# Making the source masks of an edge-count stage on GpSimd instead of VectorE

## The reference

```python
edge_index = jnp.stack([src, dst])
x = layernorm(x + L0(x, edge_index))   # encoder 1024->512->256, 3 layers with
                                       #   agg = segment_sum(h[src], dst); z = h + agg, decoder
x = layernorm(x + L1(x, src, dst))     # 2 layers: h @ W_self + (agg * deg_inv) @ W_neigh + b
```

## Time and profile before

| | |
|---|---|
| median of 3 runs | 1109.51 us (1109.46 to 1112.61) |
| the profiled execution | 1108.93 us, span 1107.1 us |
| mean granted TensorE clock | 0.959 |
| PE busy | 1019.6 us, 92% of the span |
| DVE busy | 532.7 us, 48% |
| ACT busy | 351.0 us, 32% |
| POOL busy | 260.8 us, 24% |

### The profile page before, as it was taken

One profiled execution on the slowest core, in us unless ns is written; L12 is line 12 of the kernel. 1 busy time (PEld: TensorE's weight loads), 2 busy tenths in 40 slices (PEclk: granted clock), 3 DMA queues, 4 the chain that ended last, 5 costly groups with the idle time before them and its releaser, 6 DMA issues.

```text
span 1107.1 us, 14813 instructions
## 1 busy us (share of the span) xinstructions
PE 1019.6 (92%) x4862; PEld 822.2 (74%) x4862; DVE 532.7 (48%) x1314; ACT 351.0 (32%) x632; POOL 260.8 (24%) x314
## 2 busy tenths in 40 slices
PE   4787899798988599899999999999999999999996
PEld 2455668787887478777777777778887777877775
DVE  7968674455747678633222333221334234234545
ACT  5435542233424457622111222111431101222222
POOL 3000000473222533174200706001506102400000
PEclk9688898899998799999999999999999999999998
DMA  5197754299000358431322303332533433202534
GB/s 196 39 208 155 129 142 76 93 206 194 0 21 1 134 199 276 138 118 53 122 98 98 109 0 92 115 136 72 166 108 100 145 117 117 95 1 88 178 122 135
DMA packets 48263, 127.13 MB, mean 115 GB/s; under 512 B 17775, under 2 KB 18784, under 8 KB 48016
## 3 DMA queue, kind: packets, MB, share of 16 engines
q1 hardware_dynamic: 33910, 85.18, 26.3%
q0 software_dynamic: 8000, 27.02, 9.9%
q10 hardware_dynamic: 6298, 14.21, 3.8%
HBM read 101.76 MB, written 45.13 MB: 133 GB/s over the span
## 4 chain that ended last, share of the span: by engine, by line
PE 77%; DVE 8%; ACT 5%; DMA 4%; issue 3%; SPq 1%; POOL 1%; ACTq 0%; DVEq 0%; POOLq 0%
PE bank L1693 40%; PE bank L1714 17%; PE bank L1043 5%; PE bank L1075 4%; PE bank L1400 4%; DMA x_rows<-x 4%; PE bank L613 3%; ACT xt_f L260 1%; DVE stats L380 1%; PE bank L1381 1%; PE bank L1414 1%; DMA w_f<-W_pairs 1%; DVE wide L933 1%; ACT z_new L854 1%; POOL h_f L792 1%
## 5 line engine op out<-in xcount | busy, mean ns | idle before, releaser
L1634 DVE TENSOR_TENSOR h_stage<-h_turned,h_stage 128x1000 fp32r<-128x1000 f32 x80 | 104.0, 1301 | 371.9 <-ACT h_stage L1566 371.9
L1693 PE MATMUL bank<-w_self,h_stage 128*125 128x512 f32 x960 | 230.3, 395 | 0.0
L1693 PE MATMUL bank<-w_neigh,h_stage 128*125 128x512 f32 x960 | 227.0, 396 | 3.4 <-issue 3.4
L1693 PEld LDWEIGHTS bank<-w_neigh,h_stage 128*125 128x125 f32 x960 | 177.9, 186 | 47.4 <-issue 3.6
L1693 PEld LDWEIGHTS bank<-w_self,h_stage 128*125 128x125 f32 x960 | 177.9, 185 | 45.7
L1714 PE MATMUL bank<-g_rows,a_stage 125*125 125x512 f32 x800 | 192.4, 394 | 0.0
L1566 ACT ACTIVATE h_stage<-h_turned 128x1000 fp32r (+1 forms) x80 | 83.8, 1049 | 305.9 <-PE bank L1693 293.4
L1714 PEld LDWEIGHTS bank<-g_rows,a_stage 125*125 125x125 f32 x800 | 148.3, 185 | 37.6
L1531 POOL CAST w_self<-w_stage 128x512 fp32r<-128x512 f32 x32 | 22.7, 709 | 229.3 <-PE bank L1693 221.6
L1075 PE MATMUL bank<-a_turned,gn 125*128 125x418 f32 x360 | 70.5, 354 | 2.9 <-DVE gn L937 2.4
L613 PE MATMUL bank<-xt,w 128*128 128x252 f32 x480 | 63.4, 296 | 8.2 <-ACT xt_f L260 8.2
(11 more groups left out here) (204 smaller groups left out, 1162.8 us busy)
## 6 DMA issues: line engine op xcount, KB each, us to landing
a_stage<-at_dram SPq DMA_DIRECT2D x40, 625.0 KB, 4.0
w_stage<-w_self POOLq DMA_DIRECT2D x32, 256.0 KB, 3.1
at_dram<-a_turned SPq DMA_DIRECT2D x10, 625.0 KB, 9.9
w_stage<-w_neigh POOLq DMA_DIRECT2D x24, 256.0 KB, 2.9
dec_y<-x_bd SPq DMA_DIRECT2D x10, 512.0 KB, 4.2
dec_x<-x_ob SPq DMA_DIRECT2D x10, 512.0 KB, 5.3
x_dram<-h_rows SPq DMA_DIRECT2D x10, 512.0 KB, 3.8
h_dram<-o ACTq DMA_DIRECT2D x20, 256.0 KB
```

Of the source, the lines that this page charges most:

```text
L1634: dve.tensor_tensor(st[u][:, 1, :, :], ht[:, :, bass.ds(t * NT, NT)], raw(st[u][:, 0, :, :]), ALU.subtract).then_inc(st_ready, 1)
L1693: mm = pe.matmul(out, st[u][:, a, k, :], w[:, b, k * 512:(k + 1) * 512], start=(k == 0 and p == 0), stop=(k == KD - 1 and p == 2))
```

## The change

GpSimd makes the source masks of all 175 fixed visits, with the same `tensor_scalar`, and signals each on a new semaphore `sources_ready`. VectorE makes only their destination masks. TensorE waits for both before each fixed visit. The masks of the loop `more` stay on VectorE, both kinds. The slots and the rule when one is free are as before, and GpSimd now keeps to that rule too. The identity of pair p-1 is added after the source masks of pair p (the last two pairs' one after the other at the end).

```diff
+        def visit_sources(n, g, v):
+            place_src, _, slot, freed = visit_place(n // (GROUP * STATIC), n % (GROUP * STATIC))
+            if freed:
+                pool.wait_ge(hot_free, freed)
+            pool.tensor_scalar(place_src[0:EC, slot, 0:NT], iota[0:EC, 0:NT], tab[0:EC, 1, g, v:v + 1], None, ALU.is_equal)\
+                .then_inc(sources_ready, 1)
+
+        pool.wait_ge(tab_ready, 1)
+        pool.wait_ge(visit_in, 48)
+        pool.wait_ge(places_set, 3)
+        n = 0
         for p in range(PAIRS):
-            add_eye(p)
+            for j in range(GROUP):
+                for v in range(STATIC - 1):
+                    visit_sources(n, GROUP * p + j, v)
+                    n += 1
+            for j in range(GROUP):
+                visit_sources(n, GROUP * p + j, STATIC - 1)
+                n += 1
+            if p > 0:
+                add_eye(p - 1)
+        add_eye(PAIRS - 1)
...
             if freed:
                 dve.wait_ge(hot_free, freed)
-            dve.tensor_scalar(place_src[0:EC, slot, 0:NT], iota[0:EC, 0:NT], tab[0:EC, 1, g, v:v + 1], None, ALU.is_equal)
             dve.tensor_scalar(place_keys[0:EC, slot, :], iota[0:EC, :], tab[0:EC, 0, g, v:v + 1], None, ALU.is_equal)\
                .then_inc(hot_ready, 1)
...
         def count(n, j, start, stop):
+            pe.wait_ge(sources_ready, n + 1)
             pe.wait_ge(hot_ready, n + 1)
```

More of the change, by code:

```diff
@@ L120, in graph_block @@
         sem("picks"), sem("tab_ready"))
-    hot_ready, hot_free = sem("hot_ready"), sem("hot_free")
+    hot_ready, hot_free, sources_ready = sem("hot_ready"), sem("hot_free"), sem("sources_ready")
     more_visit, more_picked, more_picks, more_tab, more_ready, more_free = (sem("more_visit"), sem("more_picked"),
```

## The result

The change makes the kernel slower. 18 runs of it have a median of 1118.62 us (1112.97 to 1125.17), 18 runs of the kernel before, made beside them, 1111.39 us (1109.46 to 1113.8): ratio 1.0066, 95% interval 1.0052 to 1.0080, so +7.3 us (5.8 to 8.9). Forecast were +5.0 us. The profiled execution took 1116.28 us with a span of 1114.5 us, 7.4 us more than before.

The account below looks back on a forecast made before the run. VectorE's chain was taken to bound pair 0, row loads pairs 1 and 2, masks pairs 3 and 4. Terms +0.3 + 0 + 2.0 + 2.2 + 0.5 = +5.0 us gave 1113.9, median 1114.5; range 1104.5 to 1124, its own 1110 to 1119.

Parts of the forecast that it names:

- GpSimd's mask: Each source mask on GpSimd: 0.53 us by itself, plus 0.16 for collisions with VectorE, a pace of 0.69 us.
- the line between one and 250 elements: Straight line between GpSimd's one-operation `tensor_scalar` times, 0.22 us and 0.84 to 0.86, giving 0.53 us for 125 elements.
- The 13th mask: Pairs 3 and 4: 13 source masks made after slots come free, 9.7 us against VectorE's 7.1 and 7.5.
- 13 x 0.16 + 0.7: Pair 3's collisions: 0.16 us for each of 13 source masks, plus 0.7 for VectorE's `norm_low`.
- Rival (c): Source mask cheap on GpSimd, 0.31 us: 1106 us with collisions, 1103.6 without; chance 0.17.
- rival (a): Full exclusion beside VectorE, 0.79 us a source mask, in pairs 0, 2, 3 and 4: +14.8 us, 1124; chance 0.20.
- The free 0.64 us: Pair 3, TensorE's idle before the matmuls of `more`: source masks up to 0.64 us late cost nothing, +2.6 becomes +2.0.
- Pair 4: 13 source masks take 9.7 against 7.5 us, with no free 0.64: +2.2 us.
- The allowance of 0.5 for a lower clock: First stage: longer gaps before `dense` may keep TensorE's clock at its lower level a little longer, +0.5 us.
- Pair 0: GpSimd's sources ready at 41.8 us, choice +0.6 at about 42.3, the last five visits -0.85 and +0.5: sum +0.3.
- Pairs 1 and 2: Last 13 source masks 2.6 us late, hidden behind the row loads: 0 us.
- the room: TensorE's idle in `dense` behind the row loads, 5.46 us in pair 1 and 2.73 in pair 2, nearly used up there.

Follow-up runs that it names:

- spare_masks: Kernel before, VectorE still making all masks, plus GpSimd making the same 175 source masks into a spare place nobody reads: +8.0 us against before, ratio 1.0072.
- deep_ring: Changed kernel with 20 instead of 12 ring slots for source masks, destination masks staying at 12: +1.4 us against before, ratio 1.0013.

## Why the prediction was right, and where it was not

The sign and the mechanism were right, and so was the place of most of the loss; +5.0 us were forecast and +7.3 measured. Step by step:

- **GpSimd's mask.** Forecast 0.53 us by itself and 0.69 with collisions. Measured 0.60 where VectorE is quiet (median of the `more_src` masks), one every 0.574 us, so the line between one and 250 elements was 0.04 us a mask too low. The 13th mask was forecast 9.7 us after the first slot and ended after 10.2 us. Of that (10.25), 13 x 0.574 are 7.46, and the other 2.8 us are collisions, where the forecast had 13 x 0.16 + 0.7 = 2.8. The collisions were right in sum, and the whole error is the mask's own price. They do not come evenly, as the forecast had them: 2.2 us stand in three masks, one of 1.35 us beside `norm_low` and two of 1.51 and 1.10 us beside VectorE's masks of `more`, while beside the destination masks one takes 0.67.
- **A cheap mask.** Rival (c) had 0.31 us, by the one row of 0.40 us for 250 elements. It is refuted for this instruction, by 0.60 us. Two columns alone take 0.28.
- **Exclusion.** In rival (a) each source mask waits out a whole destination mask and each VectorE addition whole, an assumption of mine. The 2.43 and 1.51 us masks agree with such waiting. The masks of 0.67 us beside VectorE's destination masks do not: (a) had 0.79 there, and with a mask's own pace as measured it would be 0.574 + 0.26 = 0.83. Rival (a) put the 13 masks at 11.5 us; they took 10.2. spare_masks shows what the average hides: the loser need not be GpSimd (VectorE's visit 0.61 us instead of 0.43, GpSimd's pace 0.61 instead of 0.574).
- **The free 0.64 us** was the step that failed. I took 0.64 off in pair 3, because TensorE had waited that long after the choice. After, the choice itself is longer: its products take 0.97 + 0.98 us instead of 0.57 + 0.58, and the granted clock of TensorE is 0.50 there instead of 1.00. Windows of before and after around these products (the number behind the busy times of the five engines is the granted clock):

```profile
141.20:142.20 1.00, 0.97 (x8) 0.94 (x8) 1.00 (x6) 0.00 (x0) 0.85 (x1) 1.00 1.35 534
```

```profile
145.80:147.60 1.80, 1.78 (x9) 1.79 (x10) 0.00 (x0) 0.00 (x0) 1.80 (x4) 0.50 1.26 449
```

  The granted clock is 1.00 before and 0.50 after. Ahead of them TensorE had visits with a gap of 0.2 to 1.1 us before each, where the last visits of before follow one another within 0.05 us, behind a single gap of 1.38. That the many gaps lowered the clock is my reading; no run separates it. The last two visit matmuls there take 0.60 us each instead of 0.39. So nothing was free. Pair 3 is +3.2 instead of +2.0, of which 0.64 is this step and 0.5 the dearer mask: from the last mask to the choice it takes 1.0 us before and after. Pair 4 is +2.7 instead of +2.2. The allowance of 0.5 for a lower clock ahead of `dense` was not borne out in sum: `dense` of pair 2 wins 1.5 us (granted clock 1.00 instead of 0.83), and from the choice of pair 4 to the end of the stage 0.3 us are lost. What the clock cost lies at the choice of pair 3, 0.50 against 1.00.
- **Pair 0.** Last source ready: forecast 41.8, measured 41.7. Choice: forecast 42.3, measured 42.80. From the last mask to the choice it takes 1.1 us after, as it did before (40.5 to 41.66 in the earlier trace rows, at a granted clock of 0.50 in both); I had put 0.5 there, an error of my own sum. The five last visits took back part: VectorE's statistics begin 0.3 us later than in the earlier trace rows, as forecast, but the table was ready 0.4 us earlier in this execution. Counted from the table it is +1.5 at the choice and +0.7 at the statistics, against a forecast of +0.6 and +0.3.
- **Pairs 1 and 2.** Forecast 0, with the room nearly used up in pair 2. TensorE's idle time in `dense` after:

```profile
87.77 1.44 PE L633 MATMUL bank<-xt,w 128*128 128x252 f32 x5 [4.72 <-ACT xt_f L260]
123.62 1.10 PE L633 MATMUL bank<-xt,w 128*128 128x252 f32 x7 [1.20 <-ACT xt_f L260]
```

  1.20 us is left of 2.73. The lateness was hidden, as forecast. But the rows themselves came 2.7 us later here (VectorE begins their statistics at 118.64 instead of 115.97 us), mostly by the longer loads. An estimate for loads as short as in the profile of before: TensorE reaches this wait 4.45 us later than before, 1.57 of them by the first load, so 2.88 us of a room of 2.73 + 0.43 would have been used and about 0.3 left.
- **What the prediction did not separate.** Its forecast would have been the same for any kernel with these 13 masks late. deep_ring shows that lateness, not work, is the loss in pairs 3 and 4: the same 175 masks and collisions, made earlier, cost nothing there. In pair 0, where GpSimd cannot work ahead, the collisions decide: 30 masks at 0.574 us alone, an estimate, would have been ready at 34.5 us, and were at 41.7.

By TensorE's places the two profiled executions differ by +1.4 (ahead of pair 3) + 3.2 + 2.7 + 0.3 = +7.7 us at the end of the stage, against a forecast of +0.3 + 2.0 + 2.2 + 0.5. The mis-sized terms are the mask's own price (0.04 us low, 0.5 us over 13 masks) and the 0.64 us taken for free in pair 3. Pair 0 came out as forecast at the load (+0.4), because the slip at the choice was mostly given back behind it. The other 1.0 us ahead of pair 3 is what the two long loads and the statistics took more, less the 1.5 us that `dense` of pair 2 gave back, and single profiles vary by that. That +5.0 comes as near as 2.3 us to the measured +7.3 is therefore in part luck. Neither it nor these two profiles covers the lower mean clock of 11 of the 18 executions (0.946 to 0.953).

## What to carry to other kernels

Moving work to an idle engine pays when that engine can make it ahead of need, so look first at how many slots it has, not at its share of busy time: eight more slots of 256 bytes a partition turned +7.3 us into +1.4, and leaving the urgent first masks on the fast engine made it -4.3. Before giving GpSimd work beside a VectorE that bounds, price what it does to VectorE: here a visit of 0.43 us became 0.61 even when nobody used GpSimd's result. A wait of a few tenths that ends on another engine need not be free room: here the products behind it took 0.97 us at a granted clock of 0.50 when they came late, and 0.57 at 1.00 before. And before a single profile is read as an effect, profile the unchanged kernel a second time: here its first stage alone differed by 7 us.

## What the runs showed of the hardware

- GpSimd's `is_equal` mask, 125 x 125 from 16 bit to 16 bit, takes 0.60 us (one every 0.574 us); with 2 columns it takes 0.28. VectorE's same mask takes 0.25.
- Where VectorE and GpSimd both ran short masks (`spare_masks`) they went in step: six GpSimd masks in 3.67 us, VectorE two masks each 0.61 us. In the changed kernel a GpSimd mask beside VectorE's masks of `more`, back to back, took 1.51 us; beside two VectorE additions of 1.40 and 1.21 us it took 2.43. Which of the two pays differs from place to place in that execution: beside the 1.51 us mask VectorE's first four masks for `more` kept their 0.25 and 0.34 us, while six destination masks beside GpSimd's masks of 0.67 us took 1.95 instead of 1.56 us. What decides it was not found.
- The two long row loads took 20.4 and 20.3 us in one execution of a program and 22.1 and 22.7 in another.
- The same 72 matmuls took 10.28 us at a granted clock of 0.83 and 8.75 us at 1.00, the longer time behind an idle 2.73 us of TensorE, the shorter behind 1.20.
- The first of four stages took 187.0 us in one execution of a program and 194.1 in another, and the totals differ by 1.9 us.
